# Half of an integer check moved from VectorE's maxima to ScalarE's sums of squares

## The reference

```python
xn = layernorm(x)                                # without gamma and beta
# branch 1: a memory of 128x128 that decays by 0.99 a step and takes in v k^T / 4 of the 4 sequences
r_t = q_t @ M.T;  M = 0.99 * M + outer;  s = (r @ Wo.T) * sigmoid(gate)
# branch 2: layernorm with gamma and beta, two dequantised products
h  = layernorm(xn) * gamma + beta
w1 = (fc1_q - 128) * fc1_scales                  # 512 x 2048, one scale for 128 rows of a column
w2 = (fc2_q - 128) * fc2_scales                  # 2048 x 512
z  = silu(h @ w1 + fc1_bias) @ w2 + fc2_bias
g  = silu(xn + 0.5 * z)
out = x + s * g
```

## Time and profile before

| what | us |
|---|---|
| median of 3 runs (lowest, highest) | 1252.54 (1252.32, 1252.96) |
| the profiled execution: its time | 1252.95 |
| its span, first to last instruction | 1251.1 |
| PE busy | 1186.3 (95%) |
| DVE busy | 1124.8 (90%) |
| ACT busy | 913.8 (73%) |
| POOL busy | 711.4 (57%) |

### The profile page before, as it was taken

One profiled execution on the slowest core, in us unless ns is written; L12 is line 12 of the kernel. 1 busy time (PEld: TensorE's weight loads), 2 busy tenths in 40 slices (PEclk: granted clock), 3 DMA queues, 4 the chain that ended last, 5 costly groups with the idle time before them and its releaser, 6 DMA issues.

```text
span 1251.1 us, 18966 instructions
## 1 busy us (share of the span) xinstructions
PE 1186.3 (95%) x6028; PEld 616.0 (49%) x6028; DVE 1124.8 (90%) x1965; ACT 913.8 (73%) x1590; POOL 711.4 (57%) x796
## 2 busy tenths in 40 slices
PE   2789999999999999999999999999999999999994
PEld 1344554545455554555555455454545545454551
DVE  7799899899998989999898989999898998999887
ACT  6588677777767777786777777777776777778673
POOL 6056737649273673927467383755837376492742
PEclk9799999999999999999999999999999999999997
DMA  9511030402103040120303113030210304020011
GB/s 332 178 42 34 20 83 1 102 1 57 45 9 94 1 102 1 43 60 1 102 1 81 22 30 73 1 101 1 67 35 18 85 1 101 1 55 13 24 46 35
DMA packets 41620, 65.68 MB, mean 52 GB/s; under 512 B 11696, under 2 KB 11952, under 8 KB 41008
## 3 DMA queue, kind: packets, MB, share of 16 engines
q1 hardware_dynamic: 41232, 64.36, 19.3%
q10 hardware_dynamic: 288, 0.08, 0.0%
HBM read 47.59 MB, written 16.81 MB: 51 GB/s over the span
## 4 chain that ended last, share of the span: by engine, by line
PE 78%; DVE 16%; issue 3%; ACT 1%; POOL 1%; DMA 1%; SPq 0%; DVEq 0%; ACTq 0%
PE blk L491 29%; PE blk L509 29%; PE side L451 7%; DVE blk L774 6%; PE side L476 4%; PE side L440 3%; DVE g_lo L744 3%; DVE y_split L765 2%; DVE y_split L760 2%; DVE tops L812 1%; PE side L469 1%; PE side L470 1%; PE side L468 1%; PE side L461 1%; PE side L427 1%
## 5 line engine op out<-in xcount | busy, mean ns | idle before, releaser
L774 DVE TENSOR_TENSOR blk<-blk,ratio_rows 128x512 f32<-128x512 f32 x960 | 649.3, 692 | 108.7 <-PE blk L509 97.9
L638 ACT ACTIVATE blk<-blk,ratio 128x512 f32<-128x512 f32 x768 | 508.2, 670 | 249.8 <-PE blk L491 240.2
L509 PE MATMUL blk<-w_sb,y_split 128*128 128x512 f16 x2048 | 609.0, 379 | 10.9 <-DVE y_split L765 8.1
L491 PE MATMUL blk<-h_split,q_sb 128*128 128x512 f16 x2048 | 612.8, 381 | 5.1 <-ACT blk L638 3.1
L509 PEld LDWEIGHTS blk<-w_sb,y_split 128*128 128x128 f16 x2048 | 197.1, 98 | 262.6 <-DVE blk L774 20.3
L491 PEld LDWEIGHTS blk<-h_split,q_sb 128*128 128x128 f16 x2048 | 192.9, 98 | 218.1 <-issue 36.8
L645 ACT ACTIVATE y_full<-blk,par,last 128x512 f32<-128x512 f32 x256 | 201.8, 788 | 55.0 <-PE blk L491 54.5
L1073 POOL CAST h_split<-h_full 128x512 f16<-128x512 f32 x64 | 41.0, 641 | 320.1 <-ACT h_full L593 320.0
L765 DVE SCALAR_TENSOR_TENSOR y_split<-y_full,up,y_split 128x512 f16<-128x512 f32 x256 | 214.8, 839 | 0.0
L760 DVE TENSOR_SCALAR y_split<-y_full,up 128x512 f16<-128x512 f32 x256 | 150.2, 587 | 0.0
L1117 POOL TENSOR_TENSOR z_rows<-z_rows,s_rows 128x512 f32<-128x512 f32 x62 | 93.3, 1504 | 36.2 <-ACT z_rows L664 36.2
(11 more groups left out here) (154 smaller groups left out, 1152.4 us busy)
## 6 DMA issues: line engine op xcount, KB each, us to landing
xt<-in_x SPq DMA_DIRECT2D x64, 256.0 KB, 4.7
x_again<-in_x SPq DMA_DIRECT2D x256, 64.0 KB, 1.9
out<-z_rows SPq DMA_DIRECT2D x256, 64.0 KB, 1.7
w_sb<-in_q SPq DMA_DIRECT2D x4, 1024.0 KB, 13.8
ratio_rows<-ratio_dram SPq DMA_DIRECT2D x4, 1024.0 KB, 8.8
y_split<-in_q SPq DMA_DIRECT2D x1, 1024.0 KB, 10.2
h_split<-in_q SPq DMA_DIRECT2D x1, 1024.0 KB, 12.5
z_rows<-in_q SPq DMA_DIRECT2D x1, 1024.0 KB, 14.2
```

The costliest lines, as they stand in the source:

```text
L491: mm = pe.matmul(blk[J % 2][:], q1_sb[:, g, j // 4, w, j % 4 * P:(j % 4 + 1) * P], a[:, c % 2, g, :], start=(g == 0 and n == 0), stop=(g = ...
L509: mm = pe.matmul(blk2[:, i, :], y[:, J % Y_RING, rows], w2_sb[:, j, part, :], start=(j == 0 and n == 0), stop=(j == FB - 1 and n == len(te ...
L638: act.activation(blk[J % 2][:], blk[J % 2][:], ACT.Copy, scale=ratio1[:, at:at + 1]).then_inc(blk_scaled, 1)
L774: dve.tensor_tensor(blk2[:, i, :], blk2[:, i, :], ratio2_rows[:, j, :], ALU.mult).then_inc(blk2_scaled, 1)
```

## The change

- The maxima over quarters 1 and 2 of q1 and of q2 leave VectorE. ScalarE instead takes the sum over each partition of ((q - 64)^2 / EXACT_Q) of these quarters (sum_squares), and puts it in the same column of tops. A sum that isn't over EXACT_Q shows that no integer is too large, and the flags compare it as they compared the maxima. EXACT_Q becomes 1856, with 64 as the centre.
- A new step on VectorE, size_of, makes a bound of the largest integer out of such a sum (a square root by a shift of its bits), in five small instructions, for q1's bound and for q2's.
- q1's Squares stand in ScalarE's prelude, q2's at slots 2 and 5. TensorE's turns of the tops wait for them.
- In the prelude ScalarE turns quarter 0 of q1 in one instruction. Quarter 1 is turned by VectorE, behind wqkv_lo, with a semaphore of its own (q1_second_done), for which TensorE waits at blocks 4 to 7 and GpSimd before it writes h of chunk 1.
- VectorE makes fc2's ratios in the prelude, ahead of q1's last maximum, not at slot 6.
- The last eight pieces of q1 move from slots 3, 6, ..., 24 to 4, 7, ..., 25.

```diff
-EXACT_Q = 1920.0
+EXACT_Q = 1856.0
+CENTRE = 64.0
+ROOT_BIAS = 127 << 22
...
-Q1_AT = tuple(3 + 3 * n for n in range(FB // 2))
-RATIO2_AT, TOP_Q2_AT, Q2_SCALE_AT = 6, (0, 1, 3, 5), 8
+Q1_AT = tuple(4 + 3 * n for n in range(FB // 2))
+TOP_Q2_AT, SQUARE_Q2_AT, Q2_SCALE_AT = (0, 5), (2, 5), 8
...
+        squares = xz[:].rearrange("p a h -> p (a h)").bitcast(F16)
...
-            sp.wait_ge(q1_done, FB)
+            sp.wait_ge(q1_done, FB - 4)
...
-                    pe.wait_ge(q1_done, 4 * (j // 4) + g + 1)
+                    if j // 4 == 1:
+                        pe.wait_ge(q1_second_done, 1)
+                    else:
+                        pe.wait_ge(q1_done, 4 * max(j // 4 - 1, 0) + g + 1)
...
                 pe.wait_ge(tops_made, n + 1)
+                if n == OF_Q1:
+                    pe.wait_ge(q1_squared, 2)
+                if n == OF_Q2:
+                    pe.wait_ge(q2_squared, 2)
                 pe.transpose(top_bank[n][0:32, 0:P], tops[:, n % 2, :], ident[:]).then_inc(tops_turned, 1)
...
+            def sum_squares(n, quarter, of, done):
+                act.wait_ge(tops_turned, n - 1)
+                if quarter == 2:
+                    act.wait_ge(done, 1)
+                act.activation(squares, of, ACT.Square, bias=square_shift[:, 0:1], scale=EXACT_Q ** -0.5,
+                               accum_out=tops[:, n % 2, quarter:quarter + 1]).then_inc(done, 1)
...
-            for n in range(FB // 2):
-                q1_piece(n, 1.0, minus_point[:, 0:1])
+            act.activation(q1_sb[:, :, 0, 0, :], q1_in_sb[0], ACT.Identity, bias=minus_point[:, 0:1]).then_inc(q1_done, 4)
+            act.wait_ge(shift_done, 1)
+            act.wait_ge(tops_zero, 1)
+            for quarter in (1, 2):
+                act.wait_ge(q1_in[quarter], 16)
+                sum_squares(OF_Q1, quarter, q1_in_sb[quarter].rearrange("p k n -> p (k n)"), q1_squared)
...
                     q1_piece(FB // 2 + Q1_AT.index(G), up_q1, q1_shift[:, 0:1])
+                if G in SQUARE_Q2_AT:
+                    quarter = 1 + SQUARE_Q2_AT.index(G)
+                    act.wait_ge(q2_in[quarter], 16)
+                    sum_squares(OF_Q2, quarter, q2_in_sb[:, 4 * quarter:4 * quarter + 4, :].rearrange("p j h -> p (j h)"),
+                                q2_squared)
...
+            def size_of(n):
+                at = n - OF_Q1
+                link(dve.tensor_scalar(size_q[:, at, :], top_bank[n][:, P + 1:P + 3], EXACT_Q, None, ALU.mult))
+                link(dve.tensor_scalar(size_q[:, at, :].bitcast(I32), size_q[:, at, :].bitcast(I32), 1, None,
+                                       ALU.logical_shift_right))
+                link(dve.tensor_scalar(size_q[:, at, :].bitcast(I32), size_q[:, at, :].bitcast(I32), ROOT_BIAS, None,
+                                       ALU.add))
+                link(dve.tensor_tensor(size_q[:, at, :], size_q[:, at, :], top_bank[n][:, P:P + 4:3], ALU.max))
+                link(dve.tensor_tensor(size_q[:, at, 0:1], size_q[:, at, 0:1], size_q[:, at, 1:2], ALU.max))
+                return size_q[:, at, 0:1]
...
-                link(dve.tensor_scalar(bound[:, 5:6], top_q2[:], ZERO_POINT, None, ALU.add))
+                link(dve.tensor_scalar(bound[:, 5:6], size_of(OF_Q2), ZERO_POINT, None, ALU.add))
...
-            top_of_q1(1)
             dve.wait_ge(decay_done, 1)
...
-            top_of_q1(2)
+            hold(1, s2_c, KC, FB)
+            ratios(1, ratio2, KC)
+            dve.tensor_copy(ratio2[:, (FB - 1) * KC:], held[:, 1, (FB - 1) * KC:]).then_inc(ratio2_made, 1)
             top_of_q1(3).then_inc(tops_made, 1)
...
-            link(dve.tensor_scalar(bound[:, 2:3], top_q1[:], ZERO_POINT, TOP, ALU.add, ALU.max))
+            link(dve.tensor_scalar(bound[:, 2:3], size_of(OF_Q1), ZERO_POINT, TOP, ALU.add, ALU.max))
...
+            dve.tensor_scalar(q1_sb[:, :, 1, 0, :], q1_in_sb[1], -ZERO_POINT, None, ALU.add).then_inc(q1_second_done, 1)
...
-                if G == RATIO2_AT:
-                    hold(1, s2_c, KC, FB)
...
-                for n in range(len(TOP_Q2_AT)):
-                    if G == TOP_Q2_AT[n]:
-                        top_of_q2(n)
+                if G in TOP_Q2_AT:
+                    top_of_q2(3 * TOP_Q2_AT.index(G))
...
-                    pool.wait_ge(q1_done, FB // 2)
+                    pool.wait_ge(q1_squared, 2)
+                    pool.wait_ge(q1_second_done, 1)
...
+            pool.memset(square_shift[:], -CENTRE * EXACT_Q ** -0.5).then_inc(shift_done, 1)
```

More of the change, by code:

```diff
@@ L169, in build @@
         zero_c = sb("zero_c", [P, 1], F16)
+        square_shift = sb("square_shift", [P, 1], F32)
+        size_q = sb("size_q", [P, 2, 2], F32)
         minus_point = sb("minus_point", [P, 1], F32)
@@ L275, in build @@
         q1_low_zero = sem("q1_low_zero")
-        q1_done, q1_ready = sem("q1_done"), sem("q1_ready")
+        q1_done, q1_second_done, q1_ready = sem("q1_done"), sem("q1_second_done"), sem("q1_ready")
+        shift_done, q1_squared, q2_squared = sem("shift_done"), sem("q1_squared"), sem("q2_squared")
         row_c_done = sem("row_c_done")
@@ L679, in q1_again @@
                                    bias=q1_shift[:, 0:1], scale=up_q1).then_inc(q1_wide, 1)
-            act.wait_ge(const_done, 2)
-            for n in range(FB // 2):
-                q1_piece(n, 1.0, minus_point[:, 0:1])
+            def sum_squares(n, quarter, of, done):
[4 more added lines that the diff above has]
+                               accum_out=tops[:, n % 2, quarter:quarter + 1]).then_inc(done, 1)
+            act.wait_ge(const_done, 2)
+            act.wait_ge(q1_in[0], 16)
+            act.activation(q1_sb[:, :, 0, 0, :], q1_in_sb[0], ACT.Identity, bias=minus_point[:, 0:1]).then_inc(q1_done, 4)
[4 more added lines that the diff above has]
+                sum_squares(OF_Q1, quarter, q1_in_sb[quarter].rearrange("p k n -> p (k n)"), q1_squared)
             for k in range(KC):
@@ L946, in q1_parts @@
                     g, quarter = n % 4, n // 4
+                    if n == 0:
+                        dve.wait_ge(q1_second_done, 1)
                     dve.wait_ge(q1_wide, n + 1)
@@ L983, in _ @@
                     tail_output(*at)
-                if G == RATIO2_AT:
-                    hold(1, s2_c, KC, FB)
-                    ratios(1, ratio2, KC)
-                    dve.tensor_copy(ratio2[:, (FB - 1) * KC:], held[:, 1, (FB - 1) * KC:]).then_inc(ratio2_made, 1)
-                for n in range(len(TOP_Q2_AT)):
-                    if G == TOP_Q2_AT[n]:
-                        top_of_q2(n)
+                if G in TOP_Q2_AT:
+                    top_of_q2(3 * TOP_Q2_AT.index(G))
                 if G == Q2_SCALE_AT:
```

## The result

The changed kernel takes 1255.22 us (median of 20 runs), the kernel before 1252.93 beside it (20 runs); the ratio is 1.0015, with a 95% interval of 1.0008 to 1.0022. The medians differ by 2.29 us, the ratio makes it 1.9. It is slower beyond the interval, and within the 0.2% set ahead as no change. The forecast was 1253.0, half a microsecond more than the 1252.54 that it started from.

What follows compares the result with a forecast made beforehand. The first fc2 matmul's start (53.08 us) carries the whole difference: kv 0.8 us earlier, y's high half 0.16 late, widening 0.49 late, so fc2 +0.5 and 1252.54 becomes 1253.0. Range 1252.0 to 1254.0 (0.61), wider 1250.7 to 1255.0.

Steps and rivals of the forecast that it cites:

- Part 1, the flag: VectorE's prelude: two maxima leave, ratios (2.40 us) come in; q1's flag maximum moves 1.78 us earlier, to 26.5.
- Part 1, size_of: Five linked small VectorE instructions behind q1's flag, at 0.19 to 0.20 us, add 0.98 us before kv.
- d: How much earlier VectorE releases the first kv matmul: 1.78 - 0.98 = 0.8 us, bounds 0.1 to 1.5.
- Part 2: ScalarE's prelude: one 2048-wide pass and two Squares, 2.0 us each, replace eight pieces; covered, ending at 20.7.
- The fetch (a): ScalarE's cost of fetching a Square's sum: taken as 0.1 us, between free and 0.20 us.
- Part 3: Slots 0 to 9: VectorE loses about 4.4 + 2.4 us, ScalarE takes its place; y's high half 0.16 us late.
- Part 4 and 5: size_of adds 0.98 us to q2's scale, widening 0.49 later; the rest counts nothing, the 4.92 us ratio wait going.
- The ratio wait: VectorE's 4.92 us wait for ratio rows was on the path: gain of 2.5 us, 1250.5; chance 0.09.
- Silu's table: Silu's table loads ahead of the Squares, taking 1.28 us off ScalarE's chain: 1251.7 or 1251.0; chance 0.13.
- Summing: Summing slows ScalarE's Squares in prelude and slots 2 and 5; at half rate 1257.0 to 1258.4; chance 0.09.
- The check: Square sums (about 1507 expected) exceed 1856, so 2048 extra matmuls give about 1700 us; chance 0.01.
- the clock rival: TensorE's granted clock after 53.08 comes back at another time, worth 1.8 us: 1251.2 or 1254.8; chance 0.07 for both.

Runs made afterwards that it cites:

- e2: The changed kernel with size_of in six instructions, none with two SBUF inputs or more than one element: 1254.94 us, ratio 1.0015 to the kernel before.
- e10: The changed kernel without size_of, q2's Squares at slots 0 and 1, q1's first late piece at slot 3, mix with a scalar operand: 1249.27 us, ratio 0.9965.
- e3: The changed kernel with fc2's ratios made at slot 6 again: 1254.88 us, ratio 1.0015 to the kernel before.
- e4: The changed kernel with q2's four maxima back on VectorE, Squares for q1 alone, q2's bound without size_of: 1250.66 us, ratio 0.9985 to the kernel before.
- e1: The changed kernel with q2's two Squares moved from slots 2 and 5 to slots 0 and 1: 1253.41 us, ratio 1.0005 to the kernel before.

## Why the prediction was right in its range and off in its size

- **The part that bounds, and the chain from there.** That the difference is the shift of the first fc2 matmul held to 0.26 us (1198.28 against 1198.02). From y's high half to fc2 I had 0.33 more; it is 0.38 (7.72 against 7.34).
- **Part 1, the flag.** 1.78 us forecast, 1.80 measured, and the agreement is partly luck. The ratios cost 2.91 where I had 2.40, since two of their steps took 0.45 and 0.39 us beside GpSimd in place of 0.18 and 0.17; the diagonal's stall, 0.56 in place of 0.91, took the difference back.
- **Part 1, size_of: the term that failed.** "The seven steps from 48.18 to 49.52 stand 0.19 apart, so I take 5 x 0.19 to 0.20 = 0.98." The mechanism was in the prediction just before, for the diagonal, and I priced the steps by a stretch in which GpSimd had nothing to do. For that stretch the price was right (0.97 for q2's five steps), although from 48.18 to 49.52 there are eight steps, 0.17 apart on average, and not seven. In the prelude they took 2.60, so d was -0.42, outside my bounds of 0.1 to 1.5, which had no row for these steps beside GpSimd. Against the 1.62 that size_of cost more stands 0.39 that mix, the product behind q1's scale, lost of its own stall (0.54 to 0.15). The Trainium skill has the rule that I missed, on its page "SBUF — State Buffer", section "Who interferes with whom": VectorE shares a port pair with GpSimd, and one blocks the other for a whole instruction, which concerns VectorE's instructions with two SBUF inputs and its two-port modes. e2 and e10 agree with it: the steps in the exempt forms took 0.15 us, mix 0.20 in place of 0.51.
- **Part 2.** Right: the prelude's Squares are covered, and a Square is 2.0 us. The line through my two rows gives 1.91 and not 2.0, so the number came out better than its working. The fetch (a) lies between my bounds, at 0.19 as an instruction and 0 to 0.1 on ScalarE's time.
- **Part 3, engines change places.** Right: VectorE waits 6.80 us for Silu where I had some 6, and kv to Silu is 12.95 us where the sum gave 12.68. The 0.27 is TensorE's: 0.19 of it stands before the rescale at 37.05 (3.61 us behind kv, 3.42 before the change), and the rest in the wait of 0.32 left at 40.55, less a little that ScalarE's own work gained.
- **Part 4 and 5.** The widening is bound by the scale (ScalarE waited 0.98 us for it), and the wait for the ratio rows went without gain, as e3 confirms from the other side.
- **The rivals.** The ratio wait was not on the path. Silu's table is not loaded earlier: the only loads in the first 60 us are at 1.65 and 45.09, so Square ran without one of its own. Summing doesn't slow a Square. The check stays on its fast branch (6028 matmuls as before). The clock came in at another place and in a milder form: TensorE needed 6.48 us from kv to fc1's third step where it had needed 5.81. In e4 it came in where I had it, worth some 1.4 us (1196.88 against 1198.28 from fc2 on).

One kind of stall doesn't fit the account of part 1, that a step waits for GpSimd's whole instruction. In VectorE's timeline before the change:

```profile
29.35 0.54 DVE L932 TENSOR_TENSOR mix<-pow 128x1 f32<-128x1 f32 x1
```

and in GpSimd's:

```profile
29.26 1.50 POOL L1146 TENSOR_SCALAR b_half<-b_half 128x512 f32<-128x512 f32 x1
```

mix ended 0.63 us after GpSimd's halving of b2 began, which ran on to 30.76. The 16-wide last did the same in e2 and e3 (0.64 and 0.63 us), while after the change it ended with the halving (30.59 against 30.55). Why is open; GpSimd's spans are rough in these profiles, and no run moved GpSimd's work away.

So fc2's shift is 2.04 where I had 0.5 and at most 1.4. Of the 1.55 more, 1.24 are from size_of and its neighbour, 0.27 from TensorE's rate, the rest small terms. I had set fc2 later than 55 as a sign of being wrong. It came at 54.92, but x was 0.20 us early in that execution; without that it would be 55.12. My forecast's own range (1252.0 to 1254.0) missed the time. The wider one, up to 1255.0, holds it when the difference is added to the 1252.54 that I started from (1254.4 by the ratio, 1254.8 by the medians); the 1255.22 itself lies above. That it reached so far was luck: the clock rival had widened it (1254.8), and most of what filled it was size_of.

## What to carry to other kernels

A price per step is taken from a row where the neighbouring engines do what they will do at the new place; the same five steps cost 0.97 and 2.60 us. When work moves from a full engine to one with gaps, put it into a gap that the trace shows (the 4.4 us before slot 2). A piece of work that stands behind the last gap delays everything after it on the lighter engine, as it did on the full one. And look at what the next gap waits for: in e1 the time saved on ScalarE went into a wait for TensorE. A small stall that an instruction escapes may only move to the next one, so follow the path to its end before counting the gain.

## What the runs showed of the hardware

TensorE's rate in the first slots differs from execution to execution. After kv starts it first runs at the slower of its two rates: 256-wide matmuls 0.21 us apart, 512-wide ones 0.42. Later, from the fc1 step ahead of the q job on or within that job, the 512-wide ones stand 0.21 to 0.22 apart. In the kernel after the change, in TensorE's timeline:

```profile
33.44 0.37 PE L459 MATMUL side<-wqkv_hi,g_hi 128*128 128x256 f16 x1 [4.55 <-DVE wqkv_lo L985]
...
36.81 0.63 PE L448 MATMUL side<-g_hi,wqkv_hi 128*128 128x512 f16 x1
37.23 0.63 PE L448 MATMUL side<-g_lo,wqkv_hi 128*128 128x512 f16 x1
...
38.20 0.38 PE L448 MATMUL side<-g_lo,wqkv_hi 128*128 128x512 f16 x1
38.41 0.38 PE L448 MATMUL side<-g_hi,wqkv_lo 128*128 128x512 f16 x1
```

From kv to fc1's third step it is 5.81 us before, 6.48 after, and between 5.61 and 7.11 in the other runs, with the same work. What sets the moment isn't settled by these runs; no experiment held it fixed. The column of the granted clock shows the change in some executions: after the change it is 0.50 from 28 to 36 us, 0.54 from 36 to 38 and 1.00 from 38 to 40. In others it doesn't: before the change it is 1.00 from 28 to 42. The kv job stands in this window, before (us; busy of PE, PEld, DVE, ACT, POOL; PEclk, DMA share, GB/s):

```profile
34.00:36.00 2.00, 2.00 (x11) 1.37 (x9) 1.90 (x4) 0.00 (x0) 0.00 (x0) 1.00 1.05 203
```

and after:

```profile
34.00:36.00 2.00, 2.00 (x12) 1.36 (x10) 1.76 (x10) 0.00 (x0) 0.00 (x0) 0.50 1.04 186
```

The two have 11 and 12 matmuls and the same 0.21 us between them, under a granted clock of 1.00 and of 0.50, that is 2.4 and 1.2 GHz. So at such a place the spacing of the matmuls says more than the column.
